# The edge loop of a four-layer graph network: source blocks of 256 edges, sums taken every two chunks, two filter banks

## The reference, cut to what matters

```python
h = shifted_softplus(f_ij @ Wf1 + bf1)          # one row per edge, 128 wide
W = (h @ Wf2 + bf2) * rcut_ij[:, None]          # the filters
sj, vj = xs[idx_j], xv[idx_j]                   # gathered node features, 1 + 3 parts of 128
m_s, m_v, ... = products of sj, vj, u with W    # 8 parts of 128 are used
agg = segment_sum(x_ij, idx_i, num_segments=n)  # summed by the source node
S, V = small products of agg                    # then residual and layer norm
```

## Time and profile before

| | |
|---|---|
| median of three runs | 2467.25 us |
| the profiled execution | 2449.76 us |
| its span (first to last instruction) | 2447.8 us |
| TensorE busy | 2156.4 us (88%) |
| VectorE busy | 1617.6 us (66%) |
| GpSimd busy | 1478.2 us (60%) |
| ScalarE busy | 1079.6 us (44%) |
| mean granted clock of TensorE | 0.874 |

### The profile page before, as it was taken

One profiled execution on the slowest core, in us unless ns is written; L12 is line 12 of the kernel. 1 busy time (PEld: TensorE's weight loads), 2 busy tenths in 40 slices (PEclk: granted clock), 3 DMA queues, 4 the chain that ended last, 5 costly groups with the idle time before them and its releaser, 6 DMA issues.

```text
span 2447.8 us, 39732 instructions
## 1 busy us (share of the span) xinstructions
PE 2156.4 (88%) x8111; PEld 1289.7 (53%) x8111; DVE 1617.6 (66%) x4551; ACT 1079.6 (44%) x3063; POOL 1478.2 (60%) x1794
## 2 busy tenths in 40 slices
PE   4789257746779999999999799999999999999997
PEld 3456246635666545555444555555555555555555
DVE  7992569947994051110413588888888888888885
ACT  0000057736773010000010366676666666666664
POOL 2886777776665666656650366666666666666650
PEclk8657566655657999999999899999999999999999
DMA  5212010001112121121120233333333333333331
GB/s 198 61 15 73 3 11 2 2 2 23 14 15 61 16 53 15 15 54 14 15 48 6 73 96 98 98 100 97 102 98 96 100 99 100 97 96 100 100 98 43
DMA packets 78078, 147.22 MB, mean 60 GB/s; under 512 B 28701, under 2 KB 41234, under 8 KB 77655
## 3 DMA queue, kind: packets, MB, share of 16 engines
q0 software_dynamic: 51200, 103.93, 18.1%
q1 hardware_dynamic: 23884, 37.38, 4.6%
q10 hardware_dynamic: 2946, 5.28, 0.6%
HBM read 122.99 MB, written 22.82 MB: 60 GB/s over the span
## 4 chain that ended last, share of the span: by engine, by line
PE 68%; POOL 16%; DVE 7%; issue 6%; DMA 2%; DVEq 1%; ACT 0%; SPq 0%; ACTq 0%; POOLq 0%
PE ps L770 25%; POOL pair_table L452 16%; PE ps L569 10%; PE ps L594 7%; PE ps L756 4%; PE ps L711 4%; PE ps L758 3%; PE ps L757 3%; PE ps L759 3%; PE ps L656 2%; DVE dense L1160 1%; DMA pair_table<-dense 1%; DVE adj_t L1182 1%; DVE dense L1159 1%; PE ps L688 1%
## 5 line engine op out<-in xcount | busy, mean ns | idle before, releaser
L770 PE MATMUL ps<-adj_t 128*128 128x512 f32 x1408 | 671.7, 599 | 0.0
L464 POOL DMA_INDIRECT src_table<-st_rec,st_idx x320 | 387.1, 1210 | 272.8 <-DMA st_rec<-records 180.6
L452 POOL DMA_INDIRECT pair_table<-dense x320 | 393.7, 1230 | 151.2 <-issue 96.6
L951 ACT ACTIVATE adj_t<-adj_t 128x128 f32<-128x128 f32 x1056 | 344.6, 389 | 218.2 <-DVE adj_t L1328 217.0
L511 POOL DMA_INDIRECT adj_t<-z_table,adj_t x352 | 338.3, 961 | 168.3 <-DVE adj_t L1338 79.3
L770 PEld LDWEIGHTS ps<-adj_t 128*128 128x128 f32 x1408 | 253.1, 189 | 257.1 <-issue 217.1
L655 PE MATMUL ps<-dense 128*128 128x128 bf16 x512 | 145.9, 285 | 191.1 <-DVE adj_t L1182 126.3
L656 PE MATMUL ps<-dense 128*128 128x128 f32 x1024 | 299.1, 428 | 0.0
L885 ACT ACTIVATE dense<-dense 128x128 f32<-128x128 bf16 x512 | 157.2, 307 | 246.7 <-DVE dense L1160 235.5
L656 PEld LDWEIGHTS ps<-dense 128*128 128x128 f32 x1024 | 246.1, 295 | 18.9
L1182 DVE TENSOR_TENSOR adj_t<-adj_t,ps 128x256 f32 x512 | 214.2, 418 | 27.5 <-issue 23.4
(11 more groups left out here) (217 smaller groups left out, 3578.4 us busy)
## 6 DMA issues: line engine op xcount, KB each, us to landing
src_table<-dense SPq DMA_DIRECT2D x8, 704.0 KB, 7.0
adj_t<-src_table SPq DMA_DIRECT2D x88, 64.0 KB, 1.8
adj_t<-z_table,adj_t POOLq DMA_INDIRECT x352, 3.4
pair_table<-dense POOLq DMA_INDIRECT x320, 2.6
src_table<-st_rec,st_idx POOLq DMA_INDIRECT x320, 2.6
records<-dense SPq DMA_DIRECT2D x1, 5000.0 KB
st_rec<-records POOLq DMA_DIRECT2D x80, 62.5 KB, 2.2
wring<-in_edge_attr SPq DMA_DIRECT2D x2, 1562.5 KB
```

Source lines behind the costliest of these rows:

```text
L452: g.indirect_dma_start(out=pair_tables[h], out_offset=bass.IndirectOffsetOnAxis(ap=rows_i[h][0:EP, j:j + 1].bitcast(u32), axis=0), in_=pai ...
L464: g.indirect_dma_start(out=src_table, out_offset=bass.IndirectOffsetOnAxis(ap=st_idx[0:EP, k, c:c + 1].bitcast(u32), axis=0), in_=st_rec[0 ...
L770: last = mm(bank[6 + h], oh[:, c, :], msg[:, c, h * D:(h + 1) * D], start=c == 0, stop=c == GROUP - 1)
L951: last = A(msg[:, c, (2 + k) * P:(3 + k) * P], msg[:, c, MSG:MSG + P], ACT.Copy, scale=side[:, s, c, C_Y - ATT + k:C_Y - ATT + k + 1])
```

## The change

Slots of the source sort are rounded up to 256 edges, so that a slot is two chunks. A group is still four chunks, now of two slots, each with its own offset: 168 slots (`PAIRS`), 84 groups, 336 chunks. `src_offs` holds two columns of offsets. In PSUM the pair `ps67` becomes two pairs, `sums[0]` and `sums[1]` (banks 4, 5 and 6, 7), filled in turn by chunks 0, 1 and 2, 3; the filter banks are two (2, 3) instead of four (2 to 5). filter_out of chunk n waits for the messages of n-2. The first scatter of a slot waits for the add of the slot before the last. On TensorE, filter_out(next, 0) stands before scatter 2 and filter_out(next, 1) before scatter 3. On VectorE the adds come after chunk 1 (the second slot of the group before) and after chunk 3 (the first slot of this group). The filling of src_table goes by 42 chunks instead of 44, still in 8 DMAs.

```diff
--- before.py
+++ after.py
@@ -25,22 +25,22 @@
 BUCKETS = [NT * NT] * PARTS + [NT]
 COL0 = [h * PJ for h in range(PARTS)] + [0]
 COLS = [PJ] * PARTS + [EJ]
-QUANT_LOG2 = [7] * PARTS + [9]
+QUANT_LOG2 = [7] * PARTS + [8]
 LOTS_PER_BANK = [4] * PARTS + [16]
 AB = 4
 PART_CHUNKS = 2 * AB * math.ceil((E // PARTS + NT * NT * (P - 1)) // P / (2 * AB))
 PAIR_CHUNKS = PARTS * PART_CHUNKS
 GROUP = 4
-GROUPS = (E + NT * (GROUP * P - 1)) // (GROUP * P)
-GROUPS += GROUPS % 2
+PAIRS = 4 * math.ceil((E + NT * (2 * P - 1)) // (2 * P) / 4)
+GROUPS = PAIRS * 2 // GROUP
 SRC_CHUNKS = GROUPS * GROUP
 CHUNKS = [PART_CHUNKS] * PARTS + [SRC_CHUNKS]
-SLOTS = [PART_CHUNKS] * PARTS + [GROUPS]
+SLOTS = [PART_CHUNKS] * PARTS + [PAIRS]
 PAIR_COLS, SRC_COLS = 4, 32
 STAGED = 4
 BURST = 8
 
-FILL = 44
+FILL = 42
 assert SRC_CHUNKS % FILL == 0
 
 
@@ -121,7 +121,7 @@
         pair_rows = dense[:, 14592:14592 + EJ].bitcast(i32)
         src_rows = sb("src_rows", [P, EJ], i32)[:, :]
         pair_offs = ybuf[0:1, 0:PAIR_CHUNKS].bitcast(i32)
-        src_offs = sb("src_offs", [1, P], i32)[:, :]
+        src_offs = sb("src_offs", [1, 2 * P], i32)[:, :]
         rows_i = [pair_rows[:, h * PJ:(h + 1) * PJ] for h in range(PARTS)] + [src_rows]
         offs = [pair_offs[:, h * PART_CHUNKS:(h + 1) * PART_CHUNKS] for h in range(PARTS)] + [src_offs]
         b1col = sb("b1col", [P, KT])
@@ -227,9 +227,9 @@
         stat = ybuf[:, 0:2 * NT].rearrange("p (k t) -> p k t", k=2)
         wf2_raw = T1[:, 0, 0:D]
 
-        ps = [ctx.enter_context(nc.psum_tensor(f"ps{i}", [P, 512], f32)) for i in range(6)]
-        ps67 = ctx.enter_context(nc.psum_tensor("ps67", [P, 1024], f32))
-        bank = [ps[i][:, :] for i in range(6)] + [ps67[:, 0:512], ps67[:, 512:1024]]
+        ps = [ctx.enter_context(nc.psum_tensor(f"ps{i}", [P, 512], f32)) for i in range(4)]
+        sums = [ctx.enter_context(nc.psum_tensor(f"sums{u}", [P, 1024], f32)) for u in range(2)]
+        bank = [ps[i][:, :] for i in range(4)] + [sums[u][:, h * 512:(h + 1) * 512] for u in range(2) for h in range(2)]
 
         fT_bank = bank[0].bitcast(bf16)[0:PRODUCTS * ATT, 0:D]
 
@@ -727,7 +727,7 @@
                 last.then_inc(full, 1)
 
 
-            bU, bW = bank[1], bank[2:2 + GROUP]
+            bU, bW = bank[1], bank[2:4]
 
             def attrs_T(i, s):
                 gi = 2 * i + s
@@ -750,13 +750,13 @@
                 if c == 0:
                     pe.wait_ge(hi_ready, 2 * i + s + 1)
                     pe.wait_ge(lo_ready, 2 * i + s + 1)
-                if not (isinstance(n, int) and n < GROUP):
-                    pe.wait_ge(msg_ready, n - GROUP + 1)
+                if not (isinstance(n, int) and n < 2):
+                    pe.wait_ge(msg_ready, n - 1)
                 e = slice(c * P, (c + 1) * P)
-                mm(bW[c], h_hi[:, s, e], wf2_hi, start=True, stop=False)
-                mm(bW[c], h_hi[:, s, e], wf2_lo, start=False, stop=False)
-                mm(bW[c], h_lo[:, s, e], wf2_hi, start=False, stop=False)
-                mm(bW[c], ones_r, bf2_r, start=False, stop=True).then_inc(filt_done, 1)
+                mm(bW[c % 2], h_hi[:, s, e], wf2_hi, start=True, stop=False)
+                mm(bW[c % 2], h_hi[:, s, e], wf2_lo, start=False, stop=False)
+                mm(bW[c % 2], h_lo[:, s, e], wf2_hi, start=False, stop=False)
+                mm(bW[c % 2], ones_r, bf2_r, start=False, stop=True).then_inc(filt_done, 1)
 
             def scatter(i, s, c):
                 gi = 2 * i + s
@@ -764,10 +764,11 @@
                 pe.wait_ge(msg_ready, n + 1)
                 pe.wait_ge(cmul_ready, n + 1)
                 pe.wait_ge(oh_ready, n + 1)
-                if c == 0 and not (isinstance(i, int) and gi == 0):
-                    pe.wait_ge(agg_added, gi)
+                u = 2 * gi + c // 2
+                if c % 2 == 0 and not (isinstance(u, int) and u < 2):
+                    pe.wait_ge(agg_added, u - 1)
                 for h in range(2):
-                    last = mm(bank[6 + h], oh[:, c, :], msg[:, c, h * D:(h + 1) * D], start=c == 0, stop=c == GROUP - 1)
+                    last = mm(bank[4 + 2 * (c // 2) + h], oh[:, c, :], msg[:, c, h * D:(h + 1) * D], start=c % 2 == 0, stop=c % 2 == 1)
                 last.then_inc(scat_chunk, 1)
 
             def group(i, s, one=True, two=True):
@@ -781,12 +782,12 @@
                 scatter(i, s, 1)
                 if two:
                     filter_in(i + 1, s)
+                if one:
+                    filter_out(*nxt, 0)
                 scatter(i, s, 2)
                 if one:
-                    filter_out(*nxt, 0)
+                    filter_out(*nxt, 1)
                 scatter(i, s, 3)
-                if one:
-                    filter_out(*nxt, 1)
 
             pe.wait_ge(done["l3_z"], NT)
             pe.wait_ge(l3w_ready, 2)
@@ -804,7 +805,7 @@
             group(L3_IT - 1, 1, one=False, two=False)
 
 
-            pe.wait_ge(agg_added, GROUPS)
+            pe.wait_ge(agg_added, PAIRS)
             tbank = [(bank[0], bank[1]), (bank[4], bank[5])]
             svbank, obank = (bank[2], bank[6]), (bank[3], bank[7])
 
@@ -1315,7 +1316,7 @@
             def messages(i, s, c, nxt=None):
 
                 n = GROUP * (2 * i + s) + c
-                b = bank[2 + c]
+                b = bank[2 + c % 2]
                 y = [side[:, s, c, C_Y - ATT + k:C_Y - ATT + k + 1] for k in range(3)]
                 vk = [zg[:, s, c, (1 + k) * P:(2 + k) * P] for k in range(3)]
                 dve.wait_ge(z_in[s][c], 16 * (i + 1))
@@ -1337,25 +1338,25 @@
                 dve.wait_ge(vy_chain, 2 * n + 2)
                 v.tensor_tensor(msg[:, c, P:2 * P], vy[:, c, :], b[:, 2 * P:3 * P], ALU.mult).then_inc(msg_ready, 1)
 
-            def add_sums(i, s):
-                gi = 2 * i + s
-                off = dve.value_load(src_offs[0:1, ds(gi, 1)], min_val=0, max_val=(NT - 1) * MSG)
-                dve.wait_ge(scat_chunk, GROUP * (gi + 1))
-                if isinstance(gi, int) and gi == 0:
+            def add_sums(u, k):
+
+                off = dve.value_load(src_offs[0:1, ds(u, 1)], min_val=0, max_val=(NT - 1) * MSG)
+                dve.wait_ge(scat_chunk, 2 * (u + 1))
+                if isinstance(u, int) and u == 0:
                     dve.wait_ge(agg_zero, 1)
                 else:
-                    dve.wait_ge(agg_added, gi)
+                    dve.wait_ge(agg_added, u)
                 a = agg[:, ds(off, MSG)]
-                v.tensor_tensor(a, a, ps67[:, :], ALU.add).then_inc(agg_added, 1)
+                v.tensor_tensor(a, a, sums[k][:, :], ALU.add).then_inc(agg_added, 1)
 
             def group(i, s, head=False, tail=False):
-                one_hot(i, s, 0)
-                messages(i, s, 0)
-                if not head:
-                    add_sums(i if s == 1 else i - 1, 1 - s)
-                for c in range(1, GROUP):
+                for c in range(GROUP):
                     one_hot(i, s, c)
                     messages(i, s, c, nxt=(i if s == 0 else i + 1, 1 - s) if c == 1 and not tail else None)
+                    if c == 1 and not head:
+                        add_sums(2 * (2 * i + s) - 1, 1)
+                    if c == 3:
+                        add_sums(2 * (2 * i + s), 0)
 
             hidden(0, 0)
             group(0, 0, head=True)
@@ -1365,7 +1366,7 @@
                 group(i, 1)
             group(L3_IT - 1, 0)
             group(L3_IT - 1, 1, tail=True)
-            add_sums(L3_IT - 1, 1)
+            add_sums(PAIRS - 1, 1)
```

## The result

| | changed kernel | kernel before, same chip |
|---|---|---|
| median | 2495.16 us (2489.73 to 2496.76) | 2466.41 us (2462.17 to 2467.93) |
| ratio | 1.0115, 95% interval 1.0095 to 1.0136 | |
| span of the profiled execution | 2487.9 us | 2447.8 us |

The change costs 28.7 us, 1.15%. The prediction, 2519 us and slower, has the right sign, and its range holds the result; the loss is a little over half of the 52 us forecast.

A forecast was written before the change was run, and what follows sets the result against it. TensorE bounded the loop at 11.29 us per group; VectorE would take over at 10.56 + 1.90 = 12.46. Over 83 periods that is 1034.2 against 982.2 us, 52 more: 2519 us on the median, range 2470 to 2568.

The forecast's parts named there:

- What bounded the loop before: Edge loop before the change: TensorE paces it at 11.29 us per group of four chunks, VectorE's floor only 0.73 under.
- the stretch before the add: VectorE's idle time before each add of sums: its sequencer loading the offset, 0.76 us net per add, not a scatter wait.
- floor: VectorE's least time per group in the loop before: 11.26 less a 0.70 us wait for the filter product, 10.56 us.
- Fewer chunks: Edge loop: 84 groups instead of 88, alone worth 4 x 11.29 = 45 us less at the old period.
- The faster rival: Idle time before the add is a wait for TensorE, which stays the bound: 45 us less, 2422 us; chance 10%.
- The second add: One more add per group on VectorE: 1.14 us plus 0.76 of sequencer, together 1.90 us, covered by nothing.
- The contention term: VectorE's L1336 slowed beside GpSimd: two slow chunks of four kept, taken as 0, bounds -0.44 to +0.44 us per group.
- Two filter banks, nothing: filter_out waiting for the messages of n-2 costs nothing; the rival that the banks bind: 83 us on top, 2602, 6%.
- TensorE and its clock: TensorE's clock stays 1.00 in the loop; the rival, a fall to 0.64 from new pauses: 482 us more, 2949, 4%.
- Two marks of the prediction: Signs in the changed loop: period per group 12.3 to 12.7 us, and TensorE under 95% busy.

## Why the prediction was right, and where its size was off

**What bounded the loop before: right, with less margin than read.** TensorE paced, and the stretch before the add was the sequencer's. The early load in the kernel before gave 0.07 us per group, far from 0.7, and left a real wait for the scatter in its place. The 0.62 us before L1328 in the earlier trace rows stood in only 39 of some 76 groups, with a shorter one before L1312 in 37. Over 1440 to 2300 us VectorE lost 0.61 us per group to both, from start to start, where the prediction took 0.70 from one period. Its floor was therefore 11.31 - 0.61 = 10.70 us (11.31 is the period of this window), not 10.56.

**Fewer chunks, 45 us: right.** 46.4 measured alone.

**The stretch before the add belongs to the sequencer: right, and decisive.** It stands before all 168 adds, moving the load removes it, and with it 84 us. The faster rival (45 us less, 2422) was false as a forecast for this kernel. But with both loads moved the kernel takes 2394, 56 us less, near that rival's arithmetic: 11.18 per period is close to its 11.29.

**The second add, 1.90 us per group: right to 0.1.** In the new profile the add takes 1.14 to the next instruction (1801.20 to 1802.34), and from L1339 to the add it is 1.03 on average over all 168, against the 0.97 taken from two cases.

**The contention term: this is the step whose size was off.** The prediction gave it 0, "as two slow of four is what the rows show", with -0.44 to +0.44 as its bounds. L1337 has a mean of 0.342 us where it was 0.468: 4 x (0.468 - 0.342) = 0.50 us per group less, the whole lower end and a little more. The error was to keep the old alignment for a loop whose order and period were both being changed. Of the 165 slow cases before (1440 to 2390 us) 84 lay beside L519 and 81 beside L511. For the first half the reason is shown: L519 now lies beside the add, and L1339 grows again in the run that moves it back. It would have been worth laying the two timelines over each other with the new order in mind. The second half went because L1337 starts at another moment beside L511; the last section has what the traces show of that, and why the moment matters stays open.

The other terms are small and partly cancel, so that the rest of the sum came out close is in part luck. The floor was 0.14 too low. From L1339 to both adds it is 0.13 more in sum. L1324, now slow once in two groups beside GpSimd's L488 (0.55 us at 1810.83), has a mean of 0.371, 0.026 above the 0.345 of before, so 0.10 per group more. The one-hot is 0.06 less (a mean of 0.345 after 0.360). Sum: 12.46 + 0.14 + 0.13 + 0.10 - 0.06 - 0.50 = 12.27, measured 12.20. From the first add to the last that made 1014.5 us where the prediction had 1034.2, 19.7 less. The first add also starts 14.0 us after the first one-hot instead of 18.4, which the prediction did not count. Together these are the 24 us between the forecast of 52 more and the 28 measured.

The Trainium skill, SBUF — State Buffer, section "Who interferes with whom", says that a VectorE instruction with two inputs from SBUF contends with a GpSimd instruction that reads SBUF, and that one with at most one SBUF input, outside the modes in which a single input takes both ports, does not. The runs agree on both points for L519: L1336 goes from 0.34 to 0.57 us and more beside it, the add, whose second input is PSUM, stays at 1.22. The one-hot reads one SBUF tile and is slow beside L519 in the run with both loads moved (80 of 80); whether it ran in such a mode no run here shows. The same rule doesn't tell the cases of L511 apart, below.

**Two filter banks, nothing: right.** L1328 (L1329) no longer waits for L759: 1.5 us in the whole run of the changed kernel, 1.8 us in that of the run with one add, none of it after 1440 us.

**TensorE and its clock: right.** Its clock stays 1.00 in the loop with its pauses for L1339, 47.9 us in 159 waits of at most 0.7 us (1440 to 2430 us; with the total, the times and the longest):

```profile
PE ps L756 <- DVE adj_t L1339: 47.9, 159, 0.7
```

By the rule of the Trainium skill, TensorE: Matmul & The Clock Gate, section "A second HAM failure mode: psum-queue depth-cycling", the clock would have swung; the trace doesn't bear that out here.

Two marks of the prediction were missed narrowly, both mainly by the contention term: the period is 12.20 and not 12.3 to 12.7, TensorE is 95.2% busy and not under 95%.

## What to carry to other kernels

An address that an instruction takes from a register can cost its engine the whole chain of the load, here 0.7 us of standstill, if the load stands right before its use. Place it a few instructions earlier; before adding more such instructions to an engine with little margin, do that first. The profile may name a semaphore for that gap, so compare the gap with the releaser's end and look at the sequencer's own rows. And when an order is changed, lay the timelines of the engines whose instructions slow each other down (here VectorE and GpSimd) over each other again, rather than carrying the old number of collisions over.

## What the runs showed of the hardware that was not expected

- The load of one offset into a register and the address made from it hold VectorE up by 0.74 us per add; placed earlier (behind L1304, or right behind the add before), the same load leaves 4.5 us in 154 adds.
- L1336 beside GpSimd's L511 (an indirect DMA's issue, 0.95 us) is slow in 81 of 86 cases before, yet fast in 154 of 154 in the changed kernel. Two things together tell these cases apart in all eight profiles: which of a group's four L511 it is, and when VectorE's instruction starts. Counted over 1440 to 2390 us are the one-hot, the first instruction of the messages and L1336 under their various line numbers, where they start 0.28 to 0.43 us after an L511 and L519 is not beside them. After the fourth L511 of a group, behind which GpSimd goes on with L488, they are slow in 467 of 475 cases: L1336 in the kernel before, the first instruction of the messages (L1324) with both loads moved, the one-hot in the run with one add. After the other three L511 they are slow in none of 279. In the changed kernel nothing of the kind starts at that moment: L1337 starts 0.03 to 0.16 us after the fourth L511. Why this L511 and this moment matter stays open, and no run was made for it. One case of the kernel before, first GpSimd, then VectorE:

```profile
1817.42 0.95 POOL L511 DMA_INDIRECT adj_t<-z_table,adj_t  x1 [0.30 <-issue]
```

```profile
1817.71 0.59 DVE L1336 SCALAR_TENSOR_TENSOR adj_t<-adj_t 128x128 f32<-128x128 f32 x1
```

- At equal work, TensorE's loop runs 0.22 us per group (2%) faster in the order of the changed kernel with one add per group. Which of its three differences brings this also stays open.
